# The last large aggregation of a graph network: groups of 16 slots instead of 8, with the products in SBUF instead of PSUM

## What is computed

```python
x_h = einsum('nf,hfc->nhc', x, weight)            # 6250 x 4 x 64
alpha = leaky_relu(alpha_src[row] + alpha_dst[col], 0.2)
alpha = exp(alpha - segment_max(alpha, row)[row])
alpha = alpha / segment_sum(alpha, row)[row]
out = segment_sum(alpha[:, :, None] * x_h[col], row)   # 206250 edges
```

## Time and profile before

| | us |
|---|---|
| median of 3 runs | 9118.57 (9118.34 to 9122.58) |
| the profiled execution, its span | 10110.4 |
| VectorE busy | 5594.3 (55%) |
| GpSimd busy | 5337.1 (53%) |
| TensorE busy | 2288.8 (23%) |

### The profile page before, as it was taken

How to read it: one execution, slowest core, us unless ns; L and a number is a source line. 1 busy time by engine, 2 the same in 40 slices (tenths; PEclk the granted TensorE clock), 3 DMA queues, 4 the chain that set the end, 5 groups by cost and what they waited for, 6 DMA issues and landing times. The chain is left out here.

```text
span 10110.4 us, 54577 instructions
## 1 busy us (share of the span) xinstructions
PE 2288.8 (23%) x9111; PEld 1752.0 (17%) x9112; DVE 5594.3 (55%) x8828; ACT 1093.7 (11%) x2533; POOL 5337.1 (53%) x5411
## 2 busy tenths in 40 slices
PE   2112000000000002146555512000000000129995
PEld 1111000000000001135444411000000000116663
DVE  8764588788777677523333275455656556421111
ACT  1101000000000001112222201000000000002221
POOL 0025656666676654455555345776666777542221
PEclk7555555555555555578777755555555555559997
DMA  4051333433333353411111162433333333620004
GB/s 142 22 159 50 97 82 87 122 99 98 101 101 98 102 113 74 122 23 33 29 28 28 30 172 89 109 100 92 101 98 101 106 99 99 129 97 30 30 30 117
DMA packets 458121, 869.43 MB, mean 86 GB/s; under 512 B 175134, under 2 KB 294860, under 8 KB 448192
## 3 DMA queue, kind: packets, MB, share of 16 engines
q0 software_dynamic: 239536, 575.99, 23.0%
q1 hardware_dynamic: 167648, 182.04, 6.2%
q10 hardware_dynamic: 50788, 110.02, 3.3%
HBM read 693.35 MB, written 180.71 MB: 86 GB/s over the span
## 5 line engine op out<-in xcount | busy, mean ns | idle before, releaser
L914 POOL DMA_INDIRECT agg_ring<-table,agg_idx x4320 | 4275.8, 990 | 2329.8 <-issue 1323.4
L1042 DVE TENSOR_TENSOR agg_part<-agg_ring,agg_prob 128x2048 f32 x420 | 964.4, 2296 | 631.8 <-issue 556.2
L1080 DVE TENSOR_TENSOR agg_wide<-agg_wide,agg_part 128x2048 f32<-128x2048 f32 x420 | 960.4, 2287 | 14.4
L1786 PE MATMUL dense_tp<-all_ident,dense_xn 128*128 128x128 f32 x100 | 23.9, 425 | 2570.3 <-issue 2543.7
L1408 PE MATMUL agg_hp<-agg_xt,agg_w 128*128 128x256 f32 x1600 | 446.4, 439 | 579.4 <-ACT agg_ht L1378 340.3
L2208 DVE TENSOR_TENSOR experts_h<-experts_sg,experts_hp 128x682 f32<-128x682 f32 x106 | 91.8, 866 | 779.7 <-ACT experts_sg L2191 779.7
L2158 PE MATMUL experts_hp<-mixture_w,experts_xt 128*128 x1696 | 518.2, 458 | 0.6 <-ACT experts_xt L2187 0.6
L1408 PEld LDWEIGHTS agg_hp<-agg_xt,agg_w 128*128 128x128 f32 x1600 | 352.4, 224 | 663.8 <-ACT agg_ht L1378 360.4
L1786 PEld LDWEIGHTS dense_tp<-all_ident,dense_xn 128*128 128x128 f32 x100 | 20.3, 228 | 2571.9 <-issue 2544.5
L2129 POOL DMA_INDIRECT yc<-experts_ysb,experts_list x105 | 103.7, 987 | 685.2 <-DVE experts_ysb L2217 685.2
L1422 PE MATMUL agg_yp<-agg_w,agg_ht 128*128 128x256 f32 x1600 | 405.3, 411 | 231.0 <-remote 174.5
(11 more groups left out here) (421 smaller groups left out, 6520.8 us busy)
## 6 DMA issues: line engine op xcount, KB each, us to landing
agg_ring<-table,agg_idx POOLq DMA_INDIRECT x4320
y<-agg_ysb ACTq DMA_DIRECT2D x25, 1024.0 KB
rank_y<-y SPq DMA_DIRECT2D x10, 2560.0 KB
rank_x<-x SPq DMA_DIRECT2D x30, 640.0 KB
copies<-first_sort_words SPq DMA_DIRECT2D x16, 1024.0 KB
copies<-last_sort_words ACTq DMA_DIRECT2D x16, 1024.0 KB
x<-rank_x SPq DMA_DIRECT2D x20, 640.0 KB
agg<-agg_res ACTq DMA_DIRECT2D x98, 128.0 KB
```

Source lines behind the costliest of these rows:

```text
L914: pool.indirect_dma_start(out=self.ring[:, to:to + self.RW], out_offset=None, in_=self.table, in_offset=bass.IndirectOffsetOnAxis(ap=index ...
L1042: return dve.tensor_tensor(to[:, :].rearrange("p (j h c) -> p j h c", j=UNIT, h=H), ring[:, ds(st.at(at_u), UNIT * RW)].rearrange("p (j w) ...
L1080: dve.tensor_tensor(wide[:, :], wide[:, :], part[:, :], ALU.add).then_inc(widened, 1)
```

## The change

The function is kept as `aggregate_first` for the first aggregation. The last one gets a new `aggregate`:

- `weigh` takes 16 slots, 128 x 4096 numbers. `part` and `wide` are both 128 x 4096 and both in SBUF. Each product raises `taken` by two.
- `wide` starts with 16 slots, so the fold has one more level in front, an add of 128 x 2048.
- Between a wait and the instruction that it protects, or in place of a semaphore increment, stands a `memset` of one number (`passed`), which carries the wait.
- The tiles 1 to 48 are a loop of VectorE instead of written-out code.
- A tile of the last list has at least 16 slots instead of 8 (`least`).
- In both functions the tile's sizes are stored as six 16-bit numbers instead of five 32-bit ones, the first slot as two parts.

```diff
-    UH, UC = UNIT * H, UNIT * CW
+    UH, UC = SLOTS * H, SLOTS * CW
-        wide, part, summed = s.sb("wide", [P, UC]), s.ps("part", [P, UC]), s.sb("summed", [P, CW])
+        wide, part, folded_sum = s.sb("wide", [P, UC]), s.sb("part", [P, UC]), s.sb("folded_sum", [P, CW])
...
-                        weigh(u1, nu + first, wide).then_inc(tail, 1)
-                        n0 = dve.snap(u0 + cfg.RU)
-                        n1 = dve.snap(u1 + cfg.RU)
+                        dve.memset(passed[:, 5:6], 0.0)
+                        weigh(g1, ending, wide).then_inc(tail, 1)
                         dve.wait_ge(tail, kk)
-                        dve.sem_inc(st.dve_passed, 1)
-                        with dve.Fori(n0, n1) as n:
-                            dve.wait_ge(widened, n)
-                            weigh(n, u + first, part).then_inc(taken, 1)
-                            dve.wait_ge(taken, n)
+                        dve.memset(passed[:, 0:1], 0.0)
+                        with dve.Fori(g0, g1) as g:
+                            so_far, weighed = dve.snap(g + 1), dve.snap(g * 2 + (cfg.RU + 1))
+                            dve.wait_ge(widened, so_far)
+                            dve.memset(passed[:, 6:7], 0.0)
+                            weigh(g, u, part).then_inc(taken, 2)
+                            dve.wait_ge(taken, weighed)
                             dve.tensor_tensor(wide[:, :], wide[:, :], part[:, :], ALU.add).then_inc(widened, 1)
...
+                        dve.tensor_tensor(wide[:, 0:8 * CW], wide[:, 0:8 * CW], wide[:, 8 * CW:16 * CW], ALU.add).then_inc(eighth, 1)
+                        dve.wait_ge(eighth, kk)
                         dve.tensor_tensor(wide[:, 0:4 * CW], wide[:, 0:4 * CW], wide[:, 4 * CW:8 * CW], ALU.add).then_inc(quartered, 1)
...
-        (Cfg("2", 206250, 2048, 96), a["src"], a["dst"], None, 4, 64),
+        (Cfg("2", 206250, 2048, 96, SLOTS), a["src"], a["dst"], None, 4, 64),
```

More of the change, by code:

```diff
@@ L49, with __init__ @@
 class Cfg:
-    def __init__(self, name, E, F, RS):
+    def __init__(self, name, E, F, RS, least=UNIT):
         self.name, self.E, self.F, self.RS = name, E, F, RS
+        self.least = least
         self.RING, self.RU = RS // SLOTS, RS // UNIT
@@ L631, in _ @@
                 dve.wait_ge(md_made, 1)
-                ic.link(dve, dve.tensor_scalar(mdi[:, 0:NT], near[0:1, 256 + R0:256 + R0 + NT], 1.0, float(UNIT), ALU.add, ALU.max))
+                ic.link(dve, dve.tensor_scalar(mdi[:, 0:NT], near[0:1, 256 + R0:256 + R0 + NT], 1.0, float(cfg.least), ALU.add, ALU.max))
                 ic.link(dve, dve.tensor_scalar(ng, mdi[:, 0:NT], CH, None, ALU.min))
@@ L979, in aggregate, with aggregate_first @@
+def aggregate_first(nc, cfg, H, C, table, info, ell, out, self_loop, S, beside):
     CW = H * C
@@ L986, in aggregate @@
         ring, taken = st.ring, st.taken
-        sizes = s.sb("sizes", [1, 5 * (NT + 1)], I32)
+        sizes = s.sb("sizes", [1, LOAD * (NT + 1)], mybir.dt.uint16)
+        bits, split = s.sb("bits", [1, 2 * (NT + 1)], I32), s.sem("split")
         er, m, bm, mn = s.sb("er", [P, 2 * H]), s.sb("m", [P, H]), s.sb("bm", [P, H]), s.sb("mn", [P, H])
@@ L1005, in sizes_of @@
             why = "the ranking bounds every size of a tile"
-            ng, nk, c0, k0, missing = nc.values_load_multi_w_load_instructions(sizes[0:1, ds(t * 5, 5)], engines=[eng.engine], min_val=0, max_val=cfg.max_slots,
-                                                                      skip_runtime_bounds_check_because=why)[1]
-            return nc.s_assert_within(ng, 1, CH, skip_runtime_bounds_check_because=why), nk, c0, k0, missing
+            ng, nk, c_high, c_low, k0, missing = nc.values_load_multi_w_load_instructions(
+                sizes[0:1, ds(t * LOAD, LOAD)], engines=[eng.engine], min_val=0, max_val=cfg.max_slots, skip_runtime_bounds_check_because=why)[1]
+            return nc.s_assert_within(ng, 1, CH, skip_runtime_bounds_check_because=why), nk, c_high * SLOTS + c_low, k0, missing
         with nc.Block() as block:
@@ L1027, in _ @@
                 dve.wait_ge(st.info_in, 16)
-                of_tile = sizes[:, :].rearrange("p (t w) -> p t w", w=5)
+                of_tile = sizes[:, :].rearrange("p (t w) -> p t w", w=LOAD)
+                bits2 = bits[:, :].rearrange("p (t w) -> p t w", w=2)
+                dve.tensor_scalar(bits2[:, :, 0], st.inf[:, I_C0:I_C0 + NT + 1], 4, None, ALU.logical_shift_right).then_inc(split, 1)
+                dve.tensor_scalar(bits2[:, :, 1], st.inf[:, I_C0:I_C0 + NT + 1], SLOTS - 1, None, ALU.bitwise_and).then_inc(split, 1)
                 dve.tensor_scalar(of_tile[:, :, 0], st.inf[:, I_NG:I_NG + NT + 1], 1.0, None, ALU.max).then_inc(sized, 1)
-                dve.tensor_scalar(of_tile[:, :, 4], st.inf[:, I_NK:I_NK + NT + 1], -1.0, 4096.0, ALU.mult, ALU.add).then_inc(sized, 1)
-                for w, first in ((1, I_NK), (2, I_C0), (3, I_K0)):
-                    dve.tensor_copy(of_tile[:, :, w], st.inf[:, first:first + NT + 1]).then_inc(sized, 1)
+                dve.tensor_copy(of_tile[:, :, 1], st.inf[:, I_NK:I_NK + NT + 1]).then_inc(sized, 1)
+                dve.tensor_copy(of_tile[:, :, 4], st.inf[:, I_K0:I_K0 + NT + 1]).then_inc(sized, 1)
+                dve.tensor_scalar(of_tile[:, :, 5], st.inf[:, I_NK:I_NK + NT + 1], -1.0, 4096.0, ALU.mult, ALU.add).then_inc(sized, 1)
+                dve.wait_ge(split, 2)
+                dve.tensor_copy(of_tile[:, :, 2:4], bits2[:, :, :]).then_inc(sized, 1)
                 dve.wait_ge(const, 5)
@@ L2325, in build @@
                 share = Beside([(sorts[1], 0, len(sorts[1].so.steps), 0, 17), (sorts[2], 0, EARLY, 17, NT)])
-                aggregate(nc, lists[0][0], 8, 32, tabs[0], infos[0], ells[0], outs[0], True, S, share)
+                aggregate_first(nc, lists[0][0], 8, 32, tabs[0], infos[0], ells[0], outs[0], True, S, share)
             rank(1, after=sorts[2], done=EARLY, beside=dense[1])
```

187 lines of the change are left out of this document (added).

## The result

The changed kernel takes 9571.0 us (9566.0 to 9573.8, 4 runs), the kernel before 9119.65 beside it: a ratio of 1.0495 (1.0483 to 1.0508), 451 us slower. I had said 9588. The profiled execution of the changed kernel took 9566 us by itself. The profile of the kernel before is of the upper level, that of the changed kernel of the lower one.

A forecast was written before the change was run, and what follows sets the result against it. The prediction took GpSimd's queue of 1728 gathers to bound the last aggregation, VectorE's extra work being hidden. Held gathers add 468 us and some 2 at the last tile: 9118.6 + 470 = 9588 us, range 9240 to 9695.

The forecast's parts named there:

- first add of a tile holds: Last aggregation's loop: an add at random phase holds a gather 3.80 us, 4.42 - 0.62; 49 of them, 186 us.
- a further add holds: Last aggregation's loop: each add after a tile's first holds a gather about 4.1 us; 56 of them, 230 us.
- the fold's new add holds: Fold of each tile: the new first-level add of 2.29 us holds a gather, 49 x (2.29 - 0.62) = 81 us.
- the old fold add holds less: Fold of each tile: the old 1.22 us add now falls between two gather points, saving 29 us.
- VectorE's +167 us: Last aggregation: VectorE's net extra time without the recorder, 3.4 us more a tile, all hidden behind the gathers.
- the terms that are work: VectorE, last aggregation: products +87 us, adds -16, the fold's new first level +112, memsets of one number +30.
- The mechanism: Last aggregation: a VectorE add with two SBUF inputs holds GpSimd's gather until it ends; together +468 us.
- the measured 2.02 us: Trace before, sort's words: a gather under a VectorE instruction with two SBUF inputs took 2.02 us against 0.95.
- the decisive point: In each gather, 0.13 us after its start: not passed while a two-input instruction runs; 0.82 us more needed afterwards.
- the rows of 0.7 us: Loop's register and branch rows, median 700 ns: taken as the cost of recording them, not real time.
- My estimate for the span: Profiled span of the changed kernel: 10110 + 470 - 146 = 10434 us, GpSimd's 146 us of waits saved.
- the 0.44 us gap: VectorE's gap in the first tile's code, used per loop round instead of the recorded 2.3 us; half the rounds, -46 us.

The follow-up runs named there:

- the third control: The changed kernel with the old function for the last list too, keeping only the new storage of the sizes: 10132.46 us beside 10124.35 for the kernel before.
- e4: The old function in units of 8 slots with the new sizes, `part` of the last aggregation moved to SBUF: 9449.74 us beside 9114.42 for the kernel before.
- e9: The old function in both places, `wide` in PSUM and `part` in SBUF, one reduce for three fold adds: 10091.94 us beside 10094.68 for the kernel before.
- e10: The changed kernel, its loop's add reading weights in PSUM instead of the products in SBUF: 10136.41 us beside 10124.35 for the kernel before.
- e1: The old function in units of 8 slots, new sizes, `part` of the last aggregation in SBUF: 10204.8 us beside 10095.45 for the kernel before.
- e5: The changed kernel without the loop's memset before each product: 9563.59 us beside 9114.42 for the kernel before, ratio 1.0494.

## Why the prediction was right, point by point

| step | predicted | measured |
|---|---|---|
| an instruction over 4096 numbers | 4.42 us | 4.42 |
| first add of a tile holds | 49 x 3.80 = 186 | 49 x 3.79 = 186 |
| a further add holds | 56 x 4.1 = 230 | 56 x 3.08 = 172 |
| the fold's new add holds | 49 x 1.66 = 81 | 48 x 2.00 = 96 |
| the old fold add holds less | -29 | -22 |
| all | 468 | 432, of 451 |

The -22 is what the old fold add held in the third control, at the upper level; in the changed kernel it holds nothing. That 468 lies so near 451 is in part luck: 36 us too much of holding stand against 19 us that no term has.

**The bound.** The queue of gathers sets the stage's length, and after the change it does so alone. VectorE's +167 us lay beside it: its busy time rose by 213 us from the earlier trace rows to the stretch after, as much as the terms that are work (87 - 16 + 112 + 30), and it still waited 858 us for slots. The exact match is chance: the memsets are some 350 of 0.06 us, 20 us and not 30, and the stretch before ends ahead of the last tile's last work. I had VectorE at 40 us a tile against 53.6; that it was not the bound is shown, by these waits and by the 120 us between e4 and the changed kernel.

**The mechanism** is as told, by three independent sides: the timeline of the changed kernel, e4 with nothing moved but `part`, and e9 and e10, in which adds with one SBUF input hold next to nothing. The Trainium skill's rule ("SBUF — State Buffer", Who interferes with whom), that two SBUF inputs contend with a GpSimd instruction that reads SBUF, agrees with all of them. The prediction set the measured 2.02 us against another sentence in the same place, by which a `tensor_tensor` doesn't stall the generation of descriptors. That went too far: a gather also reads its 128 indices from SBUF, so the rule may cover it already, and no run here tells which part of a gather is held. What the runs do show is that a gather as a whole stands still under such a `tensor_tensor`, for up to 4 us.

**The term that was off** is the further adds. I set the decisive point 0.13 us behind the gather's start, at 5.00 us after the last add's end, and let the next add hold it, which comes at 4.87. But the gather that starts at 4.87, within 0.02 us of the add, passes; the one after it is held, 1.25 us later, so 3.08 us are lost instead of 4.1. That is 58 us too much in the sum; the fold's add, whose phase is set by the last add too, gave 15 back.

**What is left.** 451 - 432 = 19 us, and 24 in e4. It seems to be something that both kernels share, since the 120 us between them are their held time alone. Both have the sizes in 16-bit pieces, and the control with these alone was 8 to 31 us slower. That fits, but it was measured at the other level only, the first aggregation showed none of it there, and which instructions would carry it isn't shown. The first aggregation should not move, I had said: at the lower level there is no profile of before to compare it with; it takes 2446 us in the changed kernel and 2445 in e4.

**Where I was wrong without harm.** I took the rows of 0.7 us in the sequencers' work for the cost of recording. They aren't: with no recorder the kernel before took 10069 to 10134 us beside ten of the twelve experiments, as long as its profile in the earlier trace rows, and the profile of the changed kernel, recorded like the other, has none. My estimate for the span, 10434, mixed the two levels and failed by 870 us (9564); so did the gathers' mean, 1.27 us against 1.21, whose base of 1735 us is of the upper level. The estimate for the runs stood, because I had taken the 0.44 us gap and not 2.3. That it was a fair one was luck too: nothing in it said that there are two levels, and had the pair been measured at the upper one, part of the loss would have vanished into its slack, as in e1.

## What to carry to other kernels

While GpSimd issues gathers without a pause, ask of each VectorE add whether it has two inputs in SBUF. Each such one cost the queue about its own duration less half a gather's period when it came at any phase (3.79 of 4.42 us), and 3.08 us when the loop locked the phase, whatever room VectorE had. Moving one input, or the accumulator, to PSUM avoided it, and so did a reduce from PSUM in the fold. Price a change on the engine that sets the pace, not on the one that is edited: here VectorE had room for all of its own longer work, and the time was lost on GpSimd.

## What the runs showed of the hardware that I had not expected

- The same kernel has two levels, about 9115 and 10100 us. The record names the chip of each experiment: 9, 0 and 8 for those at the upper level, 11 for e4 and e5; it names none for the pair of before and after. TensorE's mean granted clock hardly differs, 0.595 to 0.606 in the runs of the upper level and 0.601 to 0.616 in those of the lower. In profiles of the upper one the sequencer rows of VectorE, ScalarE and SyncE are often 0.7 us long (median 700 ns); in the profile of the changed kernel, on the lower one, the loop's rows are short (ns min/median/max):

```profile
L1088 DVEq FUSED_REGOPS  x105: 58/58/58, 5645.6 to 8206.9; - x105
L1088 DVEq ALU_OP  x105: 40/40/40, 5650.5 to 8216.0; - x105
L1088 DVEq COMPARE_BRANCH  x105: 43/56/63, 5650.6 to 8216.0; - x105
```

  Whether the chip makes the level, or something else that differed with it, isn't known. At the upper level a change looks smaller: `part` in SBUF costs 109 us there and 335 here. What the whole change costs there wasn't run.
- An add that starts together with a gather takes 0.02 to 0.05 us longer (4.46 us in the median of the 56 further adds instead of 4.42), while a gather that comes second waits for the add's end. It looks as if the gather's claim were short and lay at its start, and the add's lasted for its whole run; the first half of this is inferred from these few hundredths.
- The phase locks: after a tile's first add every further one held 3.07 to 3.10 us. A round of 9.3 us lets exactly five gathers end, where 7.4 would fit.
